# Rotated keys stored without their reciprocal root and scaled on GpSimd at the attention's load; tables and norm columns copied one block later

## The reference, cut to what matters

```python
q = rmsnorm(x @ Wq.T, q_norm_w)      # 32 heads; t * rsqrt(mean(t*t) + EPS) * w
k = rmsnorm(x @ Wk.T, k_norm_w)      # 8 heads
v = x @ Wv.T
q, k = rope(q, pos), rope(k, pos)    # t1*cos - t2*sin, t2*cos + t1*sin
k_all = concat(k_cache[block_table], k)   # 16 pages of 32 keys, and 32 new keys
v_all = concat(v_cache[block_table], v)
probs = softmax(where(valid, q @ k_all.T / sqrt(128), -1e30))
out = (probs @ v_all) @ Wo.T
```

## Time and profile before

| | us |
|---|---|
| median of 3 runs (2418.6 to 2423.21) | 2419.67 |
| the profiled execution | 2396.51 |
| its span | 2394.7 |
| PE busy in it | 2319.6 |
| DVE busy in it | 1855.9 |
| ACT busy in it | 1250.5 |
| GpSimd (POOL) busy in it | 486.0 |
| mean granted clock of PE, as a share of full speed | 0.989 |

### The profile page before, as it was taken

The page is one execution under the profiler, slowest core; times in us unless marked ns, Lnnn a source line. Parts: engine busy times, 40 slices in busy tenths (PEclk is TensorE's granted clock), DMA queues, the critical chain, the costliest instruction groups (busy, mean ns, idle before and its releaser), DMA issues. The chain is left out here.

```text
span 2394.7 us, 49869 instructions
## 1 busy us (share of the span) xinstructions
PE 2319.6 (97%) x15564; PEld 2101.6 (88%) x15564; DVE 1855.9 (78%) x3065; ACT 1250.5 (52%) x2438; POOL 486.0 (20%) x540
## 2 busy tenths in 40 slices
PE   5899999999879999999999999999999999999999
PEld 4687777777658999999999999999999998888877
DVE  6458988989964888888888888888888876666663
ACT  3324444444323777777777777777777771111130
POOL 0002222221102122222222222222222214132100
PEclk9999999999989999999999999999999999999999
DMA  9835656553457688888888878888788888665622
GB/s 337 280 118 105 114 105 132 107 110 77 78 136 247 232 287 302 301 297 284 292 303 296 302 279 293 304 299 296 281 296 304 299 279 288 218 217 203 220 79 106
DMA packets 683439, 545.00 MB, mean 228 GB/s; under 512 B 367700, under 2 KB 598644, under 8 KB 678772
## 3 DMA queue, kind: packets, MB, share of 16 engines
q1 hardware_dynamic: 640900, 401.07, 53.2%
q0 software_dynamic: 36864, 134.23, 15.6%
q10 hardware_dynamic: 5616, 8.93, 1.1%
HBM read 440.72 MB, written 101.27 MB: 226 GB/s over the span
## 5 line engine op out<-in xcount | busy, mean ns | idle before, releaser
L1484 DVE CUSTOM_DVE_ANT_0 at_sm<-ps,at_mask,at_factor 128x544 f32<-128x544 f32 x512 | 400.4, 782 | 205.5 <-PE ps L1378 171.6
L1412 PE MATMUL ps<-at_pt,at_v_raw 128*128 128x128 f32 x4096 | 541.0, 275 | 1.3 <-issue 1.3
L1412 PEld LDWEIGHTS ps<-at_pt,at_v_raw 128*128 128x128 f32 x4096 | 497.6, 192 | 1.8 <-issue 1.5
L1544 ACT ACTIVATE at_pt<-ps 128x512 f32<-128x512 f32 x512 | 306.0, 598 | 261.4 <-PE ps L1387 253.9
L1557 ACT ACTIVATE at_pr<-at_sm,at_nm 128x544 f32<-128x544 f32 x512 | 385.1, 752 | 38.9 <-DVE at_nm L1484 37.8
L1469 DVE TENSOR_TENSOR at_k_lo<-shared,at_k_hi 128x1088 fp32r<-128x1088 f32 x256 | 325.8, 1273 | 0.0
L1387 PE MATMUL ps<-constants,at_pr 128*128 128x128 f32 x2048 | 306.2, 272 | 0.0
L1329 POOL DMA_INDIRECT at_v_raw<-v_cache,at_idx x256 | 274.1, 1071 | 113.2 <-issue 62.1
L800 PE MATMUL ps<-xh,pr_hi 128*128 128x512 f32 x640 | 258.1, 403 | 3.5 <-DVE pr_lo L783 3.5
L1378 PE MATMUL ps<-at_k_hi,at_q_hi 128*128 128x256 f32 (+1 forms) x1024 | 253.4, 328 | 1.2 <-issue 0.6
L802 PE MATMUL ps<-xl,pr_hi 128*128 128x512 f32 x640 | 250.6, 392 | 0.0
(11 more groups left out here) (255 smaller groups left out, 4053.3 us busy)
## 6 DMA issues: line engine op xcount, KB each, us to landing
shared<-k_t SPq DMA_DIRECT2D x1024, 128.0 KB, 4.4
qk_t<-pr_turned SPq DMA_DIRECT2D x320, 128.0 KB, 2.5
shared<-qk_t SPq DMA_DIRECT2D x64, 512.0 KB, 7.3
o_t<-at_ot SPq DMA_DIRECT2D x64, 512.0 KB, 6.1
o_raw<-o_t SPq DMA_DIRECT2D x32, 1024.0 KB, 5.4
shared<-ri_d SPq DMA_DIRECT2D x32, 1024.0 KB, 7.8
f_w<-wqkv SPq DMA_DIRECT2D x12, 1024.0 KB, 5.6
s_k_in<-k_cache SPq DMA_DIRECT2D x16, 512.0 KB, 7.7
```

The source lines that it names most:

```text
L1412: e.matmul(sums(w, k), v_raw[:, q, c, g * D:(g + 1) * D], pt[:, jj % 4, c * P:(c + 1) * P], start=(k == 0 and c == 0), stop=False, skip_gr ...
L1484: e.tensor_tensor_reduce(out=sm[:, r, :], in0=scores(r), in1=mask[:, q, :], scale=factor[:, q, g:g + 1], scalar=3e38, op0=ALU.add, op1=ALU ...
L1544: e.activation(pt[:, jj % 4, :], ps_w(jj % 2), ACT.Copy).then_inc(s_pt, 1)
```

## The change

The keys are rotated and stored like the queries, without their reciprocal root. Their sums of squares go through the queries' path (`rows_of`) into a tensor of their own, and in the value steps ACT and DVE make all roots at once; SP writes the reciprocals to `inv_d`. For batches 0 and 1 DVE multiplies the new keys at the end of the projection, after it has waited for all 17 key loads of each. For the others SP loads the batch's scales, broadcast to all partitions, ahead of its pages; GpSimd waits for the loads and multiplies 128x256 behind its gathers; DVE's first split of the batch waits for that product. The copies of the tables and norm columns move from the prologue's SP queue to the feed-forward's, behind its first two loads, and ACT waits for them where the projection begins. The sine and cosine lie in `spare`.

```diff
                     if n + TB == KT:
                         inputs.load(e, dram, ("w0", "b0", "g0", "a0", "lb0"))
-                        for kind, name in enumerate(("L1_cond_q_norm_w", "L1_cond_k_norm_w")):
-                            for half in range(2):
-                                for head in range(2):
-                                    e.dma_start(wcol[head * H:(head + 1) * H, kind * 2 + half:kind * 2 + half + 1],
-                                                dram[name][half * H:(half + 1) * H].rearrange("(x o) -> x o", o=1)).then_inc(s_tab, 16)
-                        e.wait_ge(s_rope, 2)
-                        for x, table in ((cos, tables[0]), (sin, tables[1])):
-                            for first in range(2):
-                                for half in range(2):
-                                    e.dma_start(table[half * H:(half + 1) * H, first * T // 2:(first + 1) * T // 2],
-                                                x[first * H:(first + 1) * H, :]).then_inc(s_tab, 16)
                 for q in range(TB):
                     e.wait_ge(s_ko[q], 16 * KT // TB)
-                e.wait_ge(s_tab, 16 * 16)
...
             load(0)
             load(1)
+            if also:
+                also(e)
             if weights:
                 e.wait_ge(s_wl, KB)
...
-        rot, inv = cut(shared, 0, 4), cut(shared, 2048, 2)
...
-                if live(2) and j % 2 == 1 and not key(u - 2):
+                if live(2) and j % 2 == 1:
                     e.wait_ge(s_rot, pair(i, j - 2) + 1)
                     store(i, j - 2)
-                if live(4) and j % 2 == 1 and key(u - 4):
-                    e.wait_ge(s_fin, pair(i, j - 4) - QT // 2 + 1)
-                    store(i, j - 4)
-                if live(4) and (j - 4) % PER == PER - 1 and not key(u - 4):
+                if live(4) and (j - 4) % PER == PER - 1:
                     it = i + (j - 4) // PER
                     e.wait_ge(s_cs, it + 2)
                     for n in range(T // 512):
                         rows = slice(it * 8, it * 8 + 8) if static(it) else bass.ds(it * 8, 8)
-                        e.dma_start(sums_d[n:n + 1, rows, :].rearrange("o h x -> (o h) x"),
-                                    sums[n * 32:n * 32 + 8, :]).then_inc(s_cd, 16)
+                        out = ksums_d[n:n + 1, :, :] if key(u - 4) else sums_d[n:n + 1, rows, :]
+                        e.dma_start(out.rearrange("o h x -> (o h) x"), sums[n * 32:n * 32 + 8, :]).then_inc(s_cd, 16)
 
...
-                if n == 3:
-                    e.wait_ge(s_cd, 64 * (QT // PER + 1))
+                if n == 4:
+                    e.wait_ge(s_cd, 64 * (QKT // PER + 1))
                     e.dma_start(roots[:, :], sums_d.rearrange("n h x -> (n h) x")).then_inc(s_ss, 16)
+                    e.dma_start(roots_k[:, :], ksums_d.rearrange("n g x -> (n g) x")).then_inc(s_ss, 16)
+                if n == 14:
+                    e.wait_ge(s_inv, 1)
+                    for m in range(T // 512):
+                        e.dma_start(inv_d[m * NT:(m + 1) * NT, :, :].rearrange("b g s -> g b s"),
+                                    roots_k[m * HK:(m + 1) * HK, :].rearrange("g (b s) -> g b s", s=S)).then_inc(s_id, 16)
+                if n == 17:
+                    e.wait_ge(s_id, 64)
+                    e.dma_start(sums[:, :], inv_d[0:2, :, :].rearrange("(o b) g s -> o (b g s)", o=1).broadcast_to([P, 512])).then_inc(s_id, 16)
                 if c == chunks - 1 and t == 6:
                     e.wait_ge(w.s_lo, chunks * KB)
                     early.load(e, dram)
...
+            e.wait_ge(s_tab, 16 * 16)
...
             def step(i, j, u, live):
-                if live(3) and j % 2 == 0 and key(u - 3):
-                    p = pair(i, j - 3)
-                    e.wait_ge(s_bc, p - QT // 2 + 1)
-                    wait(e, s_fin, p - QT // 2 - 1)
-                    e.activation(inv[:, p % 2, :], ps[:, SUMS + p % 2, :], ACT.Sqrt, bias=cst[:, C_EPS:C_EPS + 1],
-                                 scale=1.0 / D).then_inc(s_rtk, 1)
...
                     if half == 0:
-                        if key(u) and u >= QT + NT:
-                            e.wait_ge(s_bc, p - QT // 2 - 8 + 1)
-                        elif j % 8 == 0:
+                        if j % 8 == 0:
...
-                    e.wait_ge(s_ss, 16)
-                    e.activation(roots[:, :], roots[:, :], ACT.Sqrt, bias=cst[:, C_EPS:C_EPS + 1], scale=1.0 / D).then_inc(s_root, 1)
+                    e.wait_ge(s_ss, 32)
+                    for x in (roots_k, roots):
+                        e.activation(x[:, :], x[:, :], ACT.Sqrt, bias=cst[0:x.shape[0], C_EPS:C_EPS + 1], scale=1.0 / D).then_inc(s_root, 1)
...
-                if live(3) and j % 2 == 0 and key(u - 3):
-                    p = pair(i, j - 3)
-                    q, m = p % 2, p - QT // 2
-                    e.wait_ge(s_rtk, m + 1)
-                    e.reciprocal(inv[:, q, :], inv[:, q, :]).then_inc(s_rk, 1)
-                    e.wait_ge(s_rk, m + 1)
-                    e.wait_ge(s_rot, p + 1)
-                    e.wait_ge(s_qs[q], 64 * (p // 2))
-                    for half in range(2):
-                        ins = e.tensor_tensor(turned[:, q, half, :], rot[:, 2 * q + half, :], inv[:, q, :], ALU.mult)
-                    ins.then_inc(s_fin, 1)
...
-                        if key(u):
-                            wait(e, s_fin, p - QT // 2 - 1)
-                        else:
-                            wait(e, s_qs[q], 64 * (i * (NT // 2) + j // 4))
-                        e.tensor_tensor(out(0), xcos[:, q, :], ysin[:, 0, :], ALU.subtract)
+                        wait(e, s_qs[q], 64 * (i * (NT // 2) + j // 4))
+                        e.tensor_tensor(turned[:, q, 0, :], xcos[:, q, :], ysin[:, 0, :], ALU.subtract)
                         e.wait_ge(s_e, p + 1)
-                        e.tensor_tensor(out(1), ycos[:, 0, :], xsin[:, q, :], ALU.add).then_inc(s_rot, 1)
+                        e.tensor_tensor(turned[:, q, 1, :], ycos[:, 0, :], xsin[:, q, :], ALU.add).then_inc(s_rot, 1)
...
                     w.low(e, c, k, c % 2, False)
-            e.wait_ge(s_root, 1)
+            e.wait_ge(s_root, 2)
+            e.reciprocal(roots_k[:, :], roots_k[:, :]).then_inc(s_inv, 1)
             e.reciprocal(roots[:, :], roots[:, :]).then_inc(s_inv, 1)
-            e.wait_ge(s_inv, 1)
+            e.wait_ge(s_inv, 2)
             e.transpose(roots_t[:, :], roots[:, :]).then_inc(s_inv, 1)
-            e.wait_ge(s_inv, 2)
+            e.wait_ge(s_inv, 3)
             for r in range(REP):
...
+            e.wait_ge(s_id, 80)
+            for b in range(2):
+                new = kt[:, b, NPP, :]
+                e.wait_ge(s_kp[b], 16 * (NPP + 1))
+                e.tensor_tensor(new, new, sums[:, b * HK * S:(b + 1) * HK * S], ALU.mult).then_inc(s_fixed, 1)
+            e.wait_ge(s_fixed, 2)
...
-                if live(2) and (j - 2) % 8 == 7 and not key(u - 2):
+                if live(2) and (j - 2) % 8 == 7:
...
-                if live(2) and j % 2 == 1 and key(u - 2):
-                    p = pair(i, j - 2)
-                    m = p - QT // 2
-                    if m == 0:
-                        e.wait_ge(s_cs, QT // PER + 1)
-                    wait(e, s_rtk, m - 1)
-                    e.wait_ge(s_pre, p + 1)
-                    e.matmul(ps[:, SUMS + p % 2, :], same[:, :], sqx[:, p % 8, :], start=True, stop=True).then_inc(s_bc, 1)
...
             def load_keys(b, q):
+
+                scales = inv_d[bass.ds(b, 1), :, :] if not isinstance(b, int) else inv_d[b:b + 1, :, :]
+                e.dma_start(inv[:, q, :], scales.rearrange("o g s -> o (g s)").broadcast_to([P, HK * S])).then_inc(s_kp[q], 16)
 
...
                     gather_values(q)
+                    new = kt[:, q, NPP, :]
+                    wait_apart(e, s_passed[0], (s_kp[q], (i + 1) * 16 * (NPG + 1) + 16 * NPG))
+                    e.tensor_tensor(new, new, inv[:, q, :], ALU.mult).then_inc(s_fixed, 1)
...
                     q, g, w = (jj // UB) % 2, jj % UB, (jj // 2) % 2
-                    if g == 0:
-                        e.wait_ge(s_kp[q], (i + jj // PER + 1) * 16 * NPG)
+                    if g == 0 and not (isinstance(u, int) and jj < PER):
+                        e.wait_ge(s_fixed, i * 2 + jj // UB - 1)
+                    elif g == 0:
+                        e.wait_ge(s_kp[q], 16 * NPG)
                     two = lambda x: x[:, w, :, :].rearrange("p x (n k) -> p n x k", k=PSIZE)
...
+    ksums_d = scratch("ksums_d", [T // 512, HK, 512])
+    inv_d = scratch("inv_d", [B, HK, S])
...
+        wcol = ctx.enter_context(nc.sbuf_tensor("norm_columns", [P, 4], F32))
...
-        cos, sin = (shared[:, KB * T + n * T // 2:KB * T + (n + 1) * T // 2] for n in range(2))
...
-            wcol = spare[:, 2 * T - 4:2 * T]
+            sin, cos = (spare[:, n * T // 2:(n + 1) * T // 2] for n in (2, 3))
```

(30 more changed lines are left out.)

29 lines of the change are left out of this document (14 added, 15 removed).

## The result

The changed kernel takes 2738.9 us (median of 4 runs, 2737.1 to 2740.0), the kernel before 2419.9 beside it: a ratio of 1.1315, 95% interval 1.1295 to 1.1335. The forecast was 2780, with a range of 2640 to 2880. The profiled execution took 2737.8 us with a span of 2736.0.

The account below looks back on a forecast made before the run. PE was taken to pace the attention and DVE the key stage. -49 - 5 + 23 + 391 = +360 on the profiled 2396.5 gave 2756.5 us; the median's extra 23 made 2780, range 2640 to 2880.

Parts of the forecast that it names:

- the four terms: Key stage -49, prologue -5, start of the attention +23 and the loop +391 us, together +360.
- The key stage: Key columns of the projection: less DVE work lets key pairs run at the query pairs' pace, minus 49 us.
- The prologue: Without table loads ahead, SP's last cache store goes 5 us sooner: minus 5 us, bounds nothing and 10.
- The start of the attention: DVE's wait for batch 1's last page delays row numbers, gathers and the first score operation: plus 23 us.
- PE's gap in the loop: DVE's first key split waits for GpSimd's product behind four gathers; PE stands 4.4 us in each of 62 batches.
- The clock: In the loop, PE's clock falls after each gap, costing 1.9 us a batch, bounds 0 and 2.5.
- The 23 us added at the end: Distance from the profiled execution, 2396.5, to the median, 2419.7, added to 2756.5 to give 2780 us.
- the first: Rival: in the loop PE waits as told but the clock holds, 2662 us; chance 0.15.
- the second: Rival: GpSimd's chain in the loop is longer, 62 x (5.65 + 1.9) = 468, 2857 us; chance 0.10.
- the fourth: Rival: the key stage gives nothing because SP's stores pace it, 2829 us; chance 0.04.
- the lower bound of 4.0 for the gap: Loop's low bound, 62 x 4.0 = 248 us, with no clock loss and a quick multiply.
- The third: Rival: in the loop the multiply does not hold DVE, leaving -31, 2389 us; chance 0.03.

Follow-up runs that it names:

- e6: Changed kernel with the sixteen table and norm-column loads put back into SP's prologue queue, with its wait: 2750.4 us.
- e11: The changed kernel again, unchanged, on one more chip, the one that ran the kernel before with a profile: 2739.9 us.
- e9: The kernel before, unchanged, run on one more chip with a profile of its own: 2414.0 us.
- e7: Changed kernel with DVE's products for the first two batches' new keys moved behind the attention's row numbers: 2730.7 us.
- e2: Changed kernel with GpSimd's multiply of the new keys behind two of the batch's four gathers instead of all four: 2469.5 us.
- e4: Changed kernel with a second GpSimd product of 128x256 ahead of the multiply in each batch: 2793.8 us.
- e12: Changed kernel with eight extra PE matmuls a batch, ahead of its waits for the low parts of queries and keys: 2626.5 us.
- the series: Kernels with 0, 2, 3 and 4 gathers ahead of GpSimd's multiply, 4 being the changed kernel: 2389.3, 2469.5, 2609.8 and 2738.9 us.
- e1: Changed kernel with GpSimd's multiply of the new keys ahead of all four gathers of its batch: 2389.3 us, ratio 0.9867 to the kernel before.
- e3: Changed kernel with GpSimd's multiply of the new keys behind three of the batch's four gathers: 2609.8 us.

## Why the prediction was right

The sign, the mechanism and the order of size were right; the point was 41 us too high, of which 19 lie in the four terms and 22 in the distance added to the profiled execution. By its own steps:

- **The key stage**, -48.1 for -49. The pace of the query stage holds: PE never stands, and the stores, sums and small DMAs cost nothing.
- **The prologue**, -11.7 for -5: mis-sized. The last store went at 89.5, as worked out (90), but the block ended 3 us behind it and not 6.6 as before, and the step forgot that a shorter pause is a matter of clock too. Of 11.7 us, 9.7 are the earlier start and 2.0 the first group, 3.64 us for 5.64. e6 gives 9.9 of them back. The size holds only to some us: e11 comes to this point at 98.7 and e9, before on the same chip, at 106.4, which is 7.7. The step named the bound of 10 and took 5.
- **The start of the attention**, +20.2 for +23. The landing took 2.2 us instead of 3.1, and from the row numbers to the first score operation it was 15.2 instead of 16.7. e7 won back only 8.6 of the 20.2, with a page that landed 3.7 us later.
- **PE's gap in the loop**, 4.0 us a batch for 4.4. The four gathers took 1.00, 0.94, 0.94 and 0.94 with DVE standing, and the product 0.73 for 0.74; the cast stood 5.14 us, where it was to come 5.5 late. e2 to e4 show it step by step. The term is 247 us for 62 x 4.4 = 273, the largest miss among the terms of the sum.
- **The clock**, 1.8 us a batch for 1.9 (e12: 111.8 us; the series: 114). The Trainium skill's section on oscillation (TensorE: Matmul & The Clock Gate, "HAM oscillation — how this bites in real kernels") is borne out in that every wait of 4 us costs clock too, but not in the rest: in the batch shown the burst does not start cold, since PE's first matmuls after the gap are at full pace and the slow ones begin 0.9 us behind it, and the estimate from its example, half of 1.67 us, is less than half of the 1.8 us lost. The decision to go by the earlier trace rows was right.
- **The rest of the loop.** 380.6 - 247.4 - 113 = 20 us are neither. e1's loop holds them too: it has 19 us over the first trace of before besides its wait of 9.7. Against a trace of before on its own chip (e11 and e9) the loop's difference is 1570.0 - 1208.0 = 362.0, of which 248.1 are PE's wait, and with the same 113 for the clock 1 us is left. So the 20 go with what differs between runs of before, not with the change, as far as these traces tell. That makes the nearness of +380.6 to +391 luck in part: the wait and the clock together are 361, 30 less than forecast, and 20 us that the sum does not have fill the place.
- **The 23 us added at the end** were the largest error in the point. I took the distance from the profiled execution to the median as something every kernel pays. Where it was traced (e9), it is a loss of 0.3 us a batch inside before's loop. The changed kernel's loop is set by GpSimd's chain with PE standing 4 us a batch; it took 2738.9 and 2739.9 where before took 2419.9 and 2413.7. Without the 23 the forecast is 2756.5. The same 20 us stand in the loop's line of the ledger, because it sets the changed kernel beside the fast trace of before.

Of the rivals, the first falls by e12 (the clock doesn't hold), the second by the product's 0.73 us, before which GpSimd did not stand once, the fourth by PE's 84.50 of 84.50 us in the key steps. The price of the second, 5.65 us a batch, and the lower bound of 4.0 for the gap have no working; the prediction's terms give 5.2 with a multiply of 1.3 and gathers as before, and 4.1 with the quick multiply and no hand-over. The third, the other side, was never the kernel's. e1, which moves the product ahead of the gathers by an edit, took 2389.3 us, where that rival's sum was 2389; the agreement is chance, for the prologue gave more than its -5, and the loop was not free.

## What to carry to other kernels

An operation that is put behind others in an in-order queue costs their time, not its own: here 0.73 us of arithmetic cost some 6 us a batch, 4.0 of standing and 1.8 of clock, because four gathers, some 5 us, stood ahead of it and its reader came 1.4 us after the queue woke. Ask of each new wait what is ahead of its releaser in the queue, and put what a busy engine waits for first, its loads too. And before a distance between a profiled run and a median is carried over, find the stage in which it lies.

## What was unexpected of the hardware

- The price of a gap is not in proportion to it. Gaps of 1.5, 2.7 and 4.0 us, once in a batch, cost 0.0, 1.0 and 1.84 us of clock besides in the mean. At 2.7 us it is all or nothing: of 62 nearly equal gaps 41 were followed by slow matmuls, in the batch shown 1.3 us after PE had resumed, and 21 by none (e3).
- Useless matmuls in a gap paid: eight of them a batch, 3.6 us of PE's time, made the kernel 112 us faster (e12).
- The kernel before took 2396.0, 2414.0 and 2421.0 us on three occasions, each within 0.2%, and the difference that was traced lay in its tightest loop; the changed kernel, with room in its loop, moved by 1 us.
